# First norm of a graph network: centering, squares and scaling moved from three VectorE passes to per-column ScalarE instructions

## The reference

```python
def _layernorm(x, axis=-1, eps=1e-05):
    m = jnp.mean(x, axis=axis, keepdims=True)
    v = jnp.var(x, axis=axis, keepdims=True)
    return (x - m) / jnp.sqrt(v + eps)

x = _layernorm(x + _L0_gnn_ref(x, edge_index), axis=-1)
x = _layernorm(x + _L1_gnn_ref(x, L1_gnn_W, edge_index, edge_type_8, 50000, 50000), axis=-1)
x = _layernorm(x + _L2_gnn_ref(x, src, dst, edge_weight1, ...), axis=-1)
x = _layernorm(x + _L3_gnn_ref(x, edge_index, ...), axis=-1)
```

## Time and profile before

| | us |
|---|---|
| median of 3 runs | 6080.25 |
| lowest and highest run | 6064.72, 6114.61 |
| profiled execution | 6102.17 |
| its span | 6100.4 |
| mean granted TensorE clock in it | 0.625 of 2.4 GHz |

### The profile page before, as it was taken

One profiled execution on the slowest core, in us unless ns is written; L12 is line 12 of the kernel. 1 busy time (PEld: TensorE's weight loads), 2 busy tenths in 40 slices (PEclk: granted clock), 3 DMA queues, 4 the chain that ended last, 5 costly groups with the idle time before them and its releaser, 6 DMA issues. The chain is left out here.

```text
span 6100.4 us, 69237 instructions
## 1 busy us (share of the span) xinstructions
PE 3894.4 (64%) x18482; PEld 2922.3 (48%) x18482; DVE 2443.3 (40%) x6259; ACT 1135.0 (19%) x2099; POOL 3908.8 (64%) x3584
## 2 busy tenths in 40 slices
PE   2666276767815773266665666665698677867777
PEld 2331276633305673233333333333475667656766
DVE  6999234378902225522222222222254222422236
ACT  0110011145610111111111111011254111311125
POOL 0778677757776774577777777777111777157732
PEclk9777555578965555555555555555798555665569
DMA  7004011258821224322222222222343222522246
GB/s 271 3 9 152 22 50 50 52 221 316 321 84 43 54 53 171 120 29 29 29 29 29 29 29 29 29 29 29 107 181 142 49 53 56 212 86 54 53 145 223
DMA packets 255241, 560.60 MB, mean 92 GB/s; under 512 B 82077, under 2 KB 132986, under 8 KB 240398
## 3 DMA queue, kind: packets, MB, share of 16 engines
q1 hardware_dynamic: 67235, 400.75, 17.5%
q0 software_dynamic: 156800, 104.59, 11.8%
q10 hardware_dynamic: 30954, 52.12, 2.3%
HBM read 260.04 MB, written 310.01 MB: 93 GB/s over the span
## 5 line engine op out<-in xcount | busy, mean ns | idle before, releaser
L1383 PE MATMUL e_ring<-e_msgs,e_hot 128*128 x6272 | 1387.7, 422 | 582.5 <-DVEq L1332 581.7
L1383 PEld LDWEIGHTS e_ring<-e_msgs,e_hot 128*128 128x128 f32 x6272 | 1352.0, 332 | 620.0 <-issue 620.0
L1277 POOL DMA_INDIRECT e_msgs<-y,index_D x784 | 740.0, 944 | 420.5 <-issue 225.2
L229 POOL DMA_INDIRECT e_rows<-x,e_gidx x784 | 758.7, 968 | 244.9 <-issue 238.1
L1324 DVE TENSOR_TENSOR e_hot<-e_nodes,keys_D 128x2048 f32<-128x2048 f32 x147 | 336.9, 2292 | 1103.7 <-SPq L1295 1084.6
L241 POOL DMA_INDIRECT sums<-e_total,e_sidx x392 | 637.5, 1626 | 157.6 <-issue 125.3
L1018 POOL DMA_INDIRECT list_S<-s_place,s_target x392 | 426.9, 1089 | 271.6 <-DVEq L972 152.4
L1018 POOL DMA_INDIRECT list_D<-d_place,d_target x392 | 444.7, 1135 | 167.7 <-issue 119.2
L1277 POOL DMA_INDIRECT e_msgs<-y,index_S x392 | 394.7, 1007 | 135.1 <-issue 111.2
L1277 POOL DMA_INDIRECT e_msgs<-x_by_relation,index_D x392 | 370.0, 944 | 134.4 <-issue 112.5
L1409 ACT COPY e_stage<-e_ring 128x512 f32<-128x512 f32 x196 | 114.9, 586 | 1809.1 <-PE e_ring L1383 1808.0
(11 more groups left out here) (342 smaller groups left out, 6586.5 us busy)
## 6 DMA issues: line engine op xcount, KB each, us to landing
x_by_relation<-d_stage SPq DMA_DIRECT2D x98, 1024.0 KB
agg<-e_stage ACTq DMA_DIRECT2D x196, 256.0 KB, 2.2
n_in<-agg SPq DMA_DIRECT2D x42, 896.0 KB, 6.0
n_in<-x SPq DMA_DIRECT2D x42, 896.0 KB, 5.5
sums<-zero SPq DMA_DIRECT2D x64, 393.0 KB, 5.8
x<-n_out SPq DMA_DIRECT2D x28, 896.0 KB
n_in<-sums SPq DMA_DIRECT2D x14, 1792.0 KB, 9.4
y<-n_out SPq DMA_DIRECT2D x28, 896.0 KB
```

What stands on the lines that cost most here:

```text
L229: pool.indirect_dma_start(out=rows[h][:, j, g * D:(g + 1) * D], out_offset=None, in_=table, in_offset=bass.IndirectOffsetOnAxis(ap=gidx[g] ...
L1277: pool.indirect_dma_start(out=msgs[:, (i % HELD) * D:(i % HELD + 1) * D], out_offset=None, in_=source, in_offset=bass.IndirectOffsetOnAxis ...
L1383: mm = nc.tensor.matmul(ring[:, bass.ds(bucket, D)], hot[g % 2][:, k, :], msgs[:, bass.ds(tile, D)], start=False, stop=False, skip_group_c ...
```

## The change

The subtraction, the reduction of the squares and the scaling leave VectorE. ScalarE squares each of the 28 columns with the negated mean as bias and an accumulator output that is the column's sum of squares, in two halves of 14, in slots 3 and 4, right behind its evacuations. The square root moves to slot 4. VectorE's slot 5 takes the reciprocal and the product of it and the negated mean (`shift`). ScalarE scales each column in one instruction (scale `rstd`, bias `shift`), 14 in slot 5 and 14 in slot 6. `value`, `mean` and `rstd` get two buffers, `cent` goes.

```diff
                 if n == 2:
                     dve.wait_ge(s_value, c + 1)
-                    nc.vector.tensor_reduce(mean[:, :], value[:, :, :], AX.X, ALU.add).then_inc(s_w, 1)
-                    dve.wait_ge(s_w, 3 * c + 1)
-                    nc.vector.tensor_scalar(mean[:, :], mean[:, :], 1.0 / D, None, ALU.mult).then_inc(s_w, 1)
-                if n == 3:
-                    dve.wait_ge(s_w, 3 * c + 2)
-                    if c >= 1:
-                        dve.wait_ge(s_done, c)
-                    nc.vector.tensor_tensor(cent[:, :, :], value[:, :, :], bc(mean[:, :].unsqueeze(2), [P, CH, D]),
-                                            ALU.subtract).then_inc(s_c, 1)
+                    nc.vector.tensor_reduce(mean[h][:, :], value[h][:, :, :], AX.X, ALU.add).then_inc(s_w, 1)
+                    dve.wait_ge(s_w, 2 * c + 1)
+                    nc.vector.tensor_scalar(mean[h][:, :], mean[h][:, :], -1.0 / D, None, ALU.mult).then_inc(s_w, 1)
                 if n == 5:
-                    dve.wait_ge(s_sq, c + 1)
-                    nc.vector.tensor_reduce(var[:, :], sq[:, :, :], AX.X, ALU.add).then_inc(s_var, 1)
-                if n == 6:
                     dve.wait_ge(s_std, c + 1)
-                    nc.vector.reciprocal(rstd[:, :], std[:, :]).then_inc(s_w, 1)
-                    dve.wait_ge(s_w, 3 * c + 3)
-                    if c >= 2:
-                        dve.wait_ge(s_pt, UQ * (c - 1))
-                        dve.wait_ge(s_out[h], 16 * (c // 2))
-                    nc.vector.tensor_tensor(result[h][:, :, :], cent[:, :, :],
-                                            bc(rstd[:, :].unsqueeze(2), [P, CH, D]), ALU.mult).then_inc(s_done, 1)
+                    nc.vector.reciprocal(rstd[h][:, :], std[:, :]).then_inc(s_rstd, 1)
+                    dve.wait_ge(s_rstd, 2 * c + 1)
+                    nc.vector.tensor_tensor(shift[h][:, :], mean[h][:, :], rstd[h][:, :], ALU.mult).then_inc(s_rstd, 1)
...
+            def squares(c, part):
+                h = c % 2
+                if part == 0:
+                    act.wait_ge(s_w, 2 * c + 2)
+                    if c >= 1:
+                        act.wait_ge(s_rstd, 2 * c)
+                for t in range(part * CH // 2, (part + 1) * CH // 2):
+                    op = nc.scalar.activation(sq[:, t, :], value[h][:, t, :], ACT.Square, bias=mean[h][:, t:t + 1],
+                                              accum_out=var[:, t:t + 1])
+                if part == 1:
+                    op.then_inc(s_var, 1)
+
+            def results(c, part):
+                h = c % 2
+                if part == 0:
+                    act.wait_ge(s_rstd, 2 * c + 2)
+                    if c >= 2:
+                        act.wait_ge(s_pt, UQ * (c - 1))
+                        act.wait_ge(s_out[h], 16 * (c // 2))
+                for t in range(part * CH // 2, (part + 1) * CH // 2):
+                    op = nc.scalar.activation(result[h][:, t, :], value[h][:, t, :], ACT.Identity,
+                                              scale=rstd[h][:, t:t + 1], bias=shift[h][:, t:t + 1])
+                if part == 1:
+                    op.then_inc(s_done, 1)
...
                     if s >= 1:
                         evacuate(s - 1)
+                    if c < CHUNKS and n in (3, 4):
+                        squares(c, n - 3)
                     if c < CHUNKS and n == 4:
-                        act.wait_ge(s_c, c + 1)
-                        nc.scalar.activation(sq[:, :, :], cent[:, :, :], ACT.Square).then_inc(s_sq, 1)
-                    if c < CHUNKS and n == 5:
                         act.wait_ge(s_var, c + 1)
                         nc.scalar.activation(std[:, :], var[:, :], ACT.Sqrt, scale=1.0 / D, bias=K["eps"][:, 0:1]
                                              ).then_inc(s_std, 1)
+                    if c < CHUNKS and n in (5, 6):
+                        results(c, n - 5)
```

More of the change, by code:

```diff
@@ L1447, in place_and_relate @@
         got_a = [sb(f"got_a{h}", [P, CH, D]) for h in range(2)]
-        value = sb("value", [P, CH, D])
-        cent = sb("cent", [P, CH, D])
+        value = [sb(f"value{h}", [P, CH, D]) for h in range(2)]
         sq = sb("sq", [P, CH, D])
+        shift = [sb(f"shift{h}", [P, CH]) for h in range(2)]
         result = [sb(f"result{h}", [P, CH, D]) for h in range(2)]
-        mean = sb("mean", [P, CH])
+        mean = [sb(f"mean{h}", [P, CH]) for h in range(2)]
         var = sb("var", [P, CH])
         std = sb("std", [P, CH])
-        rstd = sb("rstd", [P, CH])
+        rstd = [sb(f"rstd{h}", [P, CH]) for h in range(2)]
         xt = [sb(f"xt{h}", [P, 2, P]) for h in range(2)]
@@ L1472, in place_and_relate @@
         s_w = sem("w")
-        s_c = sem("c")
-        s_sq = sem("sq")
         s_var = sem("var")
         s_std = sem("std")
+        s_rstd = sem("rstd")
         s_done = sem("done")
@@ L1552, in norm @@
                     dve.wait_ge(s_in[h], 32 * (c // 2 + 1))
-                    if c >= 1:
-                        dve.wait_ge(s_c, c)
-                    nc.vector.tensor_tensor(value[:, :, :], got_a[h][:, :, :],
+                    if c >= 2:
+                        dve.wait_ge(s_done, c - 1)
+                    nc.vector.tensor_tensor(value[h][:, :, :], got_a[h][:, :, :],
                                             bc(K["dis"][:, c * CH:(c + 1) * CH].unsqueeze(2), [P, CH, D]), ALU.mult
@@ L1559, in norm @@
                     dve.wait_ge(s_v, c + 1)
-                    nc.vector.tensor_tensor(value[:, :, :], value[:, :, :], got_x[h][:, :, :], ALU.add
+                    nc.vector.tensor_tensor(value[h][:, :, :], value[h][:, :, :], got_x[h][:, :, :], ALU.add
                                             ).then_inc(s_value, 1)
```

## The result

| | before | after |
|---|---|---|
| median, 14 runs each | 6066.55 us | 6117.55 us |
| lowest to highest | 6053.20 to 6114.61 | 6096.09 to 6140.54 |
| ratio, 95% interval | | 1.0067 (1.0043 to 1.0091) |
| profiled execution | 6102.17 | 6118.17 |

By the ratio the change makes the kernel slower by 41 us (0.67% of 6066.55; the interval is 26 to 55 us). The medians of the two rows are 51.0 us apart and the means 40.8; the kernel before alone spreads over 61 us, so the ratio with its interval is what the text goes by. The time is inside the stated range and on the side that was forecast, by a little more than half of the forecast's 72 us.

What follows compares the result with a forecast made beforehand. GpSimd's scatters bound the stage; the chain's new period, 19.5 + 6.9 + 0.3 + 19.0 = 45.7 us, overtakes them. Stage end 1285 + 13 x 45.7 + 36.7 = 1915.8, 71.7 us later: forecast 6152 us, range 6085 to 6220.

Steps and rivals of the forecast that it cites:

- What bounds before: Stage of `place_and_relate`: ends with GpSimd's 392 scatters, 498.6 us undisturbed plus 65 us blocked; chain has 9 us a chunk spare.
- Blocking by two SBUF inputs: VectorE's long instructions with two SBUF inputs block GpSimd's scatters; removing subtraction and scaling gives 28.7 us less blocking.
- other 3.4 us a chunk: Rest of the 6.1 us a chunk removed from VectorE, on a chain with slack: worth nothing by themselves.
- The small instructions: ScalarE, slots 3 to 6: a Square with its read 0.35 us, an Identity 0.33, together 19.0 us a chunk.
- The overlap rival: Square with its read and Identity cost 0.25 us each: period 40.7 us, time 6087; chance 0.30.
- the dear one: Accumulator's read waits for its Square: pair 1.10 us, period 57.5, time 6305; chance 0.12 for everything over 6215.
- The case between rival and forecast: Only the read is hidden, second pointer counts in full (0.25 and 0.34 us): period 43.2, time 6120.
- The serial piece: Slots 0 to 3, last result to next first Square: 16.1 us at full clock, 22.6 at half, 19.5 taken.
- first target behind the start: First unit of the stage, with small instructions in its chain: first `target` about 1285 us instead of 1279.
- from last target to the end: Last unit of 28 scatters behind the last `target`: 1.1 + 28 x 1.272 = 36.7 us.
- slower 0.56: Chance that the kernel gets slower by more than about 1% (61 us), crossed at a period of 44.8 us.
- The rival on the other side: GpSimd stays the bound: small instructions 0.25 us, full clock, period 37.3; 23 us less, time 6057; chance 0.06.

Runs made afterwards that it cites:

- e3: Kernel before, with results by ScalarE (28 Identity a chunk), one wide Square of uncentred values and a VectorE reduction for their sum; ratio to before 0.9962.
- e6: e3 with TensorE's wait for the results split in two halves; ratio to before 0.996.
- e8: Kernel before, with VectorE's two long instructions (sums times degree factor, plus x) replaced by 28 short ones of 128x64; ratio to before 0.9953.
- e2: Changed kernel with half the small instructions, each Square and Identity taking two columns (half the columns normalized wrongly); ratio to before 0.998.
- e7: e6 with VectorE's two long instructions (sums times degree factor, plus x) replaced by 28 short ones of 128x64; ratio to before 0.9908.
- e4: Kernel before, with mean and reciprocal kept in PSUM instead of SBUF, leaving three product banks instead of four; ratio to before 1.0195.
- e5: Changed kernel with useless products for TensorE in its idle time, ahead of slots 4, 5, 6 and 0; ratio to before 1.001.

## Why the prediction was right or wrong

**What bounds before: right.** GpSimd's scatters bound the stage, and the chain's period counts only from somewhere between 36.0 and 40.6 us on. e3, e6, e8 and e2 have periods from 32.5 to 36.0 and end by GpSimd's sum alone: first target 31 to 33, then 498.6, then what is blocked. For e7 that is 34.0 + 1.1 + 498.6 + 9.5 = 543.2, measured 544.4.

**Blocking by two SBUF inputs: right,** as e4 (a PSUM input doesn't block) and e7 (short ones hardly do) show. In the changed kernel it fell by 19.5 us, not by 28.7, since the product behind `target` now meets the released scatter each time (14.6 us at L1555 before, 22.3 after). That was not foreseen; it cost nothing extra only because GpSimd was waiting anyway. (The prediction's "other 3.4 us a chunk" come out of no row; 6.1 less 28.7 / 13 is 3.9. Nothing rests on them.)

**The small instructions: right, and for both.** 0.33 and 0.33 us measured, 0.35 and 0.33 taken. The overlap rival (0.25 each) is refuted, and the dear one (1.10 the pair) too: the read of the accumulator is 0.20 us long, but the next Square starts 0.10 us behind the read's start. The case between rival and forecast, with the read hidden, had a period of 43.2 and a time of 6120, and measured are 43.4 and 6117.55. That is chance: the read is not hidden, and its time came back elsewhere in the sum. The Trainium skill ("ScalarE: Activation LUTs", section "What ACT_TABLE_LOAD costs") has the figures from which the prediction worked out 0.24 us for one pointer and 0.33 for two. The trace agrees: 0.24 us from a Square to its read, 0.33 from one Identity to the next.

**The serial piece: the step that was mis-sized.** "In the new loop TensorE idles about 3 us in each of slots 4 to 6, so slots 0 and 1 will mostly run slow: I take 19.5." Measured are 17.8 us (43.4 - 25.6). Three things go into that.

- The step was taken 13 times alike. Between the first two chunks the piece is 14.2 us long, between the last two 15.3, and between the others 17.5 to 18.8, on average 18.5. The first and the last period are 37.9 and 40.4 us, and that alone is 13 of the 30 us by which 13 periods of 45.7 are too long.
- The clock was sized right, but in other slots. Slots 0 and 3 run slow, not 0 and 1. The middle pieces are 18.1 to 18.8 us where both bursts are slow, 17.5 where only slot 0's is, and in e5 15.2 where none is. So the half clock costs up to 3.6 us a chunk, against 19.5 - 16.1 = 3.4 in the forecast. Which burst is slow can't be read from the idle time ahead of it alone: in the earlier trace rows the burst at 1441.86 stands behind 2.97 us and takes 1.99, and the one at 1540.38 above stands behind 2.34 and takes 3.68.
- The piece at the full clock was too dear, 16.1 us against 15.2. With the clock's share this makes 1.0 us in each of the eleven middle units, together 10 us.

The rest, 7 us, is ScalarE's own run in these eleven units: 25.6 us from first Square to last result against 6.9 + 0.3 + 19.0 = 26.2. Together the period was forecast as 45.7 and is 43.4 on average.

| term, us | forecast | measured |
|---|---|---|
| first target behind the start | 37.7 (1285 - 1247.3) | 36.5 |
| 13 periods | 594.1 | 563.9 |
| from last target to the end | 36.7 | 36.0 |
| stage | 668.5 | 636.3 |

The sum of the three differences is the stage's 32 us, and the rest of the kernel's forecast followed from it (72 against 41). In absolute time the forecast, 6152, lies 34 us over the measured 6117.55; 14 of these come from the base, 6080.25 as median of three runs against 6066.55 of fourteen. The side and the mechanism were right; the chances were on the wrong side of 1%: "slower 0.56" needed a period over 44.8, which a difference of 1.4 us a chunk decided. A step with 13 repeats makes a threshold of that kind, and the range of one guess (16.1 to 22.6) spanned 85 us of it.

**The rival on the other side,** GpSimd as the bound, did not come about. Its price, 23 us, is near what e3 and e6 with the same two passes off VectorE gained (23 and 24), but not by the same sum, so the match is in part luck: the forecast was 28.7 us of blocking less a first target 6 us later, and e3 has 22.0 us less blocking and a first target 0.8 us later, which makes its stage 20.6 us shorter.

## What to carry to other kernels

Before work is moved to an idle engine, count its new queue in the chain's terms: 19 us more for ScalarE in a period of 31.5 was no matter of busy shares (59% before), but of what stands behind it, and the slack (9 us a chunk) had to be compared with it. Where GpSimd issues indirect DMAs beside VectorE, look at which VectorE instructions have two large SBUF inputs and are long; cutting them into short ones gained here at least as much as moving them, with nothing added to another engine's queue. Small per-column instructions cost by their number: half of them, or one wide instruction plus a reduction, turned a loss of 41 us into a gain. Before a step is multiplied by its repeats, look whether the first and the last repeat are like the others: here they were 4 to 6 us shorter than the rest, and that was almost half of the error.

## What the runs showed of the hardware

- ScalarE's accumulator output is a second instruction, ACTIVATION_READ_ACCUMULATOR, of 0.19 to 0.22 us; it starts 0.24 us behind a Square of 128x64 and the next Square starts 0.33 us behind the first. A Square of this size without the accumulator was not run.
- A scatter beside 28 VectorE instructions of two SBUF inputs, each 0.20 us from start to start (2.88 us for 14), loses 0.02 us on average and 0.11 at most; beside one of 2.02 us up to 1.8 (2.75 us long). Beside one of 2.02 us with its second, small input in PSUM it loses at most 0.02, and a gather beside one of 2.29 us with an input in PSUM as little.
- TensorE's clock was granted at 0.75 of 2.4 GHz in a stage where TensorE idled 2 to 6 us several times a period; useless products in these gaps brought it to 0.93 and made the kernel 0.6% faster than without them (ratio to before 1.001 against 1.0067).
- With three product banks instead of four, and mean and reciprocal in PSUM, the same stage went from 597 to 711 us, at a granted clock of 0.61.
